# Graph network with sorted edges: digit counts before the first sort, pair counts behind it, a sixth of the records gathered later, and radial products over 128 rows

## The chip, the cores and the metric

One core of one Trainium2 chip. The time is that of one launch on the device in microseconds (us), the median of the runs shown. PE is TensorE, DVE VectorE, ACT ScalarE, POOL GpSimd, SP SyncE; SP issues most DMAs, POOL the indirect ones (gathers).

## What is computed

Four layers over a graph of 12,500 nodes with 32 features and 400,000 edges (src, dst). Each adds its result to x and normalizes the rows:

```python
edge_index = jnp.stack([src, dst])
x = _layernorm(x + gat(x, edge_index, w, fc_w, fc_b, bias))               # layer 0: attention, 4 heads
x = _layernorm(x + ratio(x, node_vec1, W, b, edge_index))                 # layer 1: weighted sums over edges
x = _layernorm(x + equivariant(x, edge_weight, edge_attr_3, edge_index))  # layer 2: radial weights per edge
x = _layernorm(x + gcn(x, edge_index, W1, b1, W2, b2))                    # layer 3: two convolutions
```

Layer 0 takes, for each edge, a logit from both ends, its maximum and sum over all edges of one src, and sums messages by src. Layer 2 computes for each edge a vector of 384 radial weights,

```python
R = jax.nn.relu(abs_distances[:, None] @ w1 + b1) @ w2 + b2   # 400,000 x 64 @ 64 x 384
```

multiplies it with spherical harmonics of the edge's vector and the features of its src, and sums by dst.

## The kernel before

Nodes are numbered in 98 windows (W) of 128 (the low 7 bits of a node number are its lane, the higher ones its window). Edges are brought into orders in which each tile of 128 edges has one window, so that sums over edges are matmuls with one-hot matrices. The kernel makes these orders itself, with six sorts of 128 x 4096 keys or of chunks, one before the gathers and five beside them:

1. `pair_counts` (DVE L1299 to L1329, PE L968 to L990): how many edges go from each window to each other. A step takes 16 columns of edges; DVE makes two one-hot tiles of 128 x 1568 for it (L1311), PE multiplies 16 pairs of 128 x 98 (L977) and adds one count to the semaphore `pairs_used`. Two buffers; DVE waits for `pairs_used` before it writes a buffer again. There are 196 steps. Then `window_tables` (PE L991) turns counts into the window of each group of edges: `win_src`, `win_nbr`, `win_dst` and `win_att`.
2. `source_list`: the first sort, by src. It inserts pads by `wpads` and needs the counts by source window alone.
3. Payloads of edges, weights, and the first node table `tab0` (37 columns), which SP sends to DRAM (`send_table(0)`, L491).
4. `id_list` (a sort), then `edge_list` 0 and 1, each one large sort and one of chunks. In a sort DVE compares and exchanges (L1449, L1450), and takes tiles that PE turned (L1016) out of the banks (L1492, L1514, L1517). PE adds one count to `turned_out` per 16 tiles.
5. Beside step 4: POOL gathers `tab0` rows of each edge's dst (L666, `gat<-tab,nbr`), 104 iterations of 4 slots of 8 gathers. ACT stores what came.
6. `segment_max` on DVE, with PE's turned tiles (L1056, L1714); then SP's wait for `seg_done` is over.
7. The attention pass, 416 steps (PE L1100, L1085, L1091; DVE L1843, L1817, L1862), and beside it POOL collects the records of edges in the order by dst (L645, `pay<-records`), 104 iterations of 4 x 8 gathers, where SP stores each slot to `by_dst` and loads the next numbers (L528, L530). Round 0 is issued ahead of `segment_max`, round 1 waits for `seg_done`.
8. Layer 1; then the radial pass, 416 steps: POOL gathers 8 tiles of features (L666, `gat<-tab,pay`) when SP has loaded the slot's `pay` from `by_dst` (the load waits for `step_done`), and computes geometry (L704 to L739); PE makes the hidden layer (L1195), ACT applies relu (L953) into `dsts`, PE multiplies by `w2p` (L1213), four times a pair of tiles in a step, DVE multiplies and reduces (L2086, L2091, L2097), PE sums (L1085).
9. Layer 3, with spreads and sums by edge lists.

Each engine runs its own program in the order in which it is written.

Of the kernel before, what the change touches and what calls it, by code (L numbers as in the profile page):

```python
# [14 lines left out]
P = 128  # L15
# [24 lines left out]
NT = NG * TILES_PER_GROUP  # L40
ROWS = P * NT

# [22 lines left out]
BLOCKS = M // GROUP  # L65
assert XROWS * M == CHUNKS * CHUNK_EDGES and QROWS * M == P * NT and XGPS * XTILES == TPS
# [9 lines left out]
HT = 16  # L76
BIG = float(2.0 ** 100)
# [62 lines left out]
def resnorm_gnn_kernel(nc, a, out):  # L140

    ctx = ExitStack()
    with ctx:
# [6 lines left out]
        def dram(name, shape):  # L150
# [34 lines left out]
                     for k in range(2)] for b in range(2)]  # L185
        pairs = [acc[0:W, k * W:(k + 1) * W] for k in range(2)]
# [21 lines left out]
        tmpi = sb("tmpi", [P, 1], I32)  # L208
        signs = sb("signs", [P, 7])
# [23 lines left out]
        pay = sb("pay", [P, SLOTS, TPS, 6])  # L233
        gat = sb("gat", [P, SLOTS, TPS, C0])
# [32 lines left out]
        hid = dsts[0:HID + 1, 0:2 * TPS * P].bitcast(F32).rearrange("p (b t n) -> p b t n", b=2, t=TPS)  # L267
# [16 lines left out]
        w2p = sb("w2p", [HID + 1, 384])  # L284
# [47 lines left out]
        consts = sem("consts")  # L332
        pairs_hot = sem("pairs_hot")
# [125 lines left out]
        def _(sp):  # L459
# [72 lines left out]
            def record_loads():  # L532
                with sp.Fori(1, ITERS) as i:
                    record_round(i, False, False)
                record_round(ITERS, False, True)

            def edge_loads(pas):
                with sp.Fori(0, ITERS) as i:
                    for s in range(SLOTS):
                        tiles = bass.ds(i * (SLOTS * TPS) + s * TPS, TPS)  # L540

                        sp.wait_ge(step_done, i * SLOTS + (BASE[pas] + s + 1))
                        sp.dma_start(payv(s, pas), by_dst_v[:, tiles, :]).then_inc(pay_in[s], 16)

            sp.wait_ge(listed, 1)
# [4 lines left out]
            send_table(0, tab0, C0)  # L550
            sp.wait_ge(listed, 2)
            sp.dma_start(ids_dst, sortA[:, 0:NT].bitcast(I32)).then_inc(ids_sent, 16)
            for k in range(2):
                sp.wait_ge(row_keys_made, k + 1)
                sp.dma_start(key_rows[k].rearrange("(p g) c -> p (g c)", p=P), row_keys).then_inc(row_keys_sent, 16)
            for s in range(SLOTS):
                sp.wait_ge(adst_out[s], 16 * ITERS)
            sp.wait_ge(row_keys_made, 3)
            sp.dma_start(arena[:, 0:NT * HEADS], adst_tiles).then_inc(seg_loaded, 16)
            sp.wait_ge(ids_sent, 16)  # L560
            record_round(0, True, False)
# [5 lines left out]
            for s in range(SLOTS):  # L567
                sp.wait_ge(rec_out[s], 16 * ITERS)
            edge_loads(PASS_L2)
# [19 lines left out]
        def _(pool):  # L589
# [44 lines left out]
            def collect():  # L634
# [16 lines left out]
                with pool.Fori(1, ITERS) as i:  # L651
                    step(i, False)

# [88 lines left out]
            def radial_gather():  # L742

                def step(i, s, gathers, geo):
# [16 lines left out]
                with pool.Fori(0, ITERS - 1) as i:  # L761
# [207 lines left out]
        def _(pe):  # L969
# [21 lines left out]
            def window_tables():  # L991
                pe.wait_ge(grouped, 1)
                t_.matmul(bank[2][0:W, 0:4], before[0:W, 0:W], wcount[0:W, :], start=True, stop=True).then_inc(ended, 1)
                for turn, lists in enumerate(((0, 1, 2), (3,))):
                    pe.wait_ge(compared, turn + 1)
                    b = 0
                    for k in lists:
                        parts = gge[k].shape[1] // (P * 3)
                        q = gge[k].shape[1] // parts
                        for part in range(parts):  # L1000
                            last = t_.matmul(bank[b][0:1, 0:q], ones[0:W, 0:1], gge[k][0:W, part * q:(part + 1) * q],
                                             start=True, stop=True)
                            b += 1
                    last.then_inc(tabled, 1)
# [33 lines left out]

            pair_counts()
            window_tables()  # L1040
            sort_turns(0, sortA, sortB, LOGM, QROWS, TILES_PER_GROUP)
# [163 lines left out]
            def radial_step(i, s, first, more):  # L1205
                n = i * SLOTS + s
                for p in range(TPS // 2):
# [4 lines left out]
                    for h in range(2):  # L1212
                        last = t_.matmul(bank[1 + 2 * (p % 2) + h][:, 0:384], hid[:, s % 2, 2 * p + h, :], w2p[:, :],  # L1213
# [29 lines left out]
        def _(dve):  # L1243
# [19 lines left out]
            dve.sem_inc(pairs_used, 2)  # L1263
            dve.sem_inc(spread_hot, SLOTS)
# [7 lines left out]
            v.memset(b1col[:, :], 1.0)  # L1272
            v.memset(prev_key[:, :], -1)
# [12 lines left out]
            v.tensor_copy(lanes[:, 0:1], lane[:, :])  # L1286
            v.tensor_scalar(wkey[:, 0:1], lane[:, :], 17, None, ALU.logical_shift_left)
# [9 lines left out]
            dve.drain()  # L1297

# [31 lines left out]

            def window_tables():
# [13 lines left out]
                v.tensor_reduce(wtotal[0:W, 3:4], pairs[0], AX.X, ALU.add)  # L1345
                dve.drain()
                for k, size in enumerate((P, P, GROUP, GROUP)):
                    v.tensor_scalar(wgroups[0:W, k:k + 1], wtotal[0:W, k:k + 1], float(size - 1), None, ALU.add)
# [844 lines left out]
```

## Time and profile before

| | |
|---|---|
| runs | 29,038.42, 29,043.08, 29,071.11 us (median 29,043.08) |
| profiled execution | 29,032.15 us, span 29,030.3 us |
| PE busy | 11,866.2 us (41%) |
| DVE busy | 17,276.3 us (60%) |
| POOL busy | 15,318.8 us (53%) |
| ACT busy | 4,732.5 us (16%) |
| mean granted clock of PE | 0.544 |

A row of a timeline gives start, duration, engine, line, operation, output and inputs with shapes, the count, and in brackets the idle time before it with what ended it. A row of stages gives its stretch, its length, busy time and number of instructions of each engine, the granted clock of PE (1.00 is 2.4 GHz, 0.50 is 1.2 GHz), the DMA share and GB/s. "remote" is a releaser outside the profile's engines and queues.

### The profile page before, as it was taken

Reading aid. Unit: us, or ns where it says so; the run is one execution under the profiler, and the core shown is the slowest. Engines: PE = TensorE matmul, PEld = TensorE weight load, DVE = VectorE, ACT = ScalarE, POOL = GpSimd, SP = SyncE. Lnnn points to the kernel's source line nnn. Section 1 sums busy time; section 2 is a strip of 40 time slices with the busy share of each in tenths; the row PEclk is TensorE's granted clock in tenths of the full one; section 3 lists DMA queues with packets and bytes.
Section 4 is the critical chain, followed back from the end, with each engine's and each line's share of the span. In section 5 each row is a group of like instructions: output and inputs, shape, how many; then the busy total and the mean of one; then the engine's idle time right before and its main releaser. Section 6 shows DMA issues by size and latency. Waiting matters only on the chain.

```text
span 29030.3 us, 271981 instructions
## 1 busy us (share of the span) xinstructions
PE 11866.2 (41%) x59822; PEld 8687.7 (30%) x59823; DVE 17276.3 (60%) x25029; ACT 4732.5 (16%) x11144; POOL 15318.8 (53%) x16979
## 2 busy tenths in 40 slices
PE   4000010000000000277743239999999996424422
PEld 3000010000000000266632125555555554313311
DVE  9986875774300000266634558888888886554555
ACT  0000000000000000022232004434434434201400
POOL 0028886876577777500002656666666662364166
PEclk9555555555555555577755555555555555555555
DMA  0011112112000000011155230000000004523623
GB/s 7 0 36 26 26 25 29 25 25 37 15 7 7 7 7 7 11 25 25 25 116 125 65 53 10 9 9 9 9 9 9 9 9 103 142 61 73 187 61 57
DMA packets 1778830, 1089.15 MB, mean 38 GB/s; under 512 B 930123, under 2 KB 1730348, under 8 KB 1777324
## 3 DMA queue, kind: packets, MB, share of 16 engines
q0 software_dynamic: 454272, 410.40, 9.6%
q1 hardware_dynamic: 827516, 358.86, 5.0%
q10 hardware_dynamic: 496944, 318.82, 4.7%
q8 instruction: 32, 0.52, 0.0%
q14 instruction: 66, 0.54, 0.0%
HBM read 697.54 MB, written 387.81 MB: 37 GB/s over the span
## 4 chain that ended last, share of the span: by engine, by line
PE 28%; another core or an unknown queue 15%; issue 13%; POOL 13%; DVE 13%; DMA 5%; DVEq 5%; ACT 3%; ACTq 3%; SPq 1%; POOLq 0%
PE banks L1213 16%; POOL gat L666 11%; PE banks L1085 9%; DMA dsts<-key_rows 3%; DVE hot L1806 3%; DVE arena L1817 2%; POOL srcs L686 2%; DVEq L450 2%; ACT dsts L953 2%; ACT srcs L883 1%; DVE arena L1449 1%; DVE arena L1311 1%; PE banks L1195 1%; DVE msg L1862 1%
## 5 line engine op out<-in xcount | busy, mean ns | idle before, releaser
L686 POOL DMA_INDIRECT srcs<-spread,nbx x2808 | 3086.2, 1099 | 6742.4 <-issue 4503.1
L666 POOL DMA_INDIRECT gat<-tab,nbr x3328 | 4074.2, 1224 | 3079.8 <-DMA tab<-arena 1926.8
L1213 PE MATMUL banks<-w2p,dsts 65*128 65x384 f32 x6656 | 4773.3, 879 | 597.7 <-ACT dsts L953 594.8
L666 POOL DMA_INDIRECT gat<-tab,pay x3328 | 3210.0, 965 | 2351.4 <-DMA pay<-by_dst 1410.1
L645 POOL DMA_INDIRECT pay<-records,nbr x3328 | 3530.7, 1061 | 1372.2 <-issue 1097.4
L1817 DVE TENSOR_TENSOR arena<-arena,banks 128x96 f32 (+3 forms) x6136 | 1539.5, 251 | 4376.3 <-remote 2516.0
L1016 PE MATMUL banks<-ident,arena 128*128 128x128 f32 x2240 | 425.9, 376 | 5679.4 <-DVE arena L1450 4555.1
L1213 PEld LDWEIGHTS banks<-w2p,dsts 65*128 65x128 f32 x6656 | 2013.1, 332 | 1895.1 <-issue 1201.6
L1085 PE MATMUL banks<-srcs,hot 128*128 128x96 bf16 (+1 forms) x11232 | 1165.2, 280 | 3425.5 <-DMA srcs<-spread,nbx 1746.8
L2097 DVE TENSOR_REDUCE red<-srcs 128x80 f32<-128x1280 f32 x1664 | 2474.5, 1487 | 151.8 <-issue 0.5
L1449 DVE TENSOR_TENSOR arena<-arena 128x1024 f32<-128x1024 f32 (+3 forms) x1548 | 2087.9, 1349 | 219.6 <-issue 149.0
L1016 PEld LDWEIGHTS banks<-ident,arena 128*128 128x128 f32 x2240 | 399.4, 202 | 5706.5 <-DVE arena L1450 4571.6
L1450 DVE TENSOR_TENSOR arena<-arena 128x1024 f32<-128x1024 f32 (+3 forms) x1548 | 2097.4, 1355 | 0.0
L1085 PEld LDWEIGHTS banks<-srcs,hot 128*128 128x128 bf16 x11232 | 872.1, 136 | 3718.7 <-DVE hot L1806 1614.9
L1898 DVE TENSOR_SCALAR hotT<-dsts,lanes 128x1024 bf16<-128x1024 uint8 x1404 | 1057.1, 753 | 1390.2 <-DMA dsts<-key_rows 1248.0
L1100 PE MATMUL banks<-nodesp,hotT 128*128 x3328 | 242.1, 174 | 3764.1 <-issue 2528.7
L1165 PE MATMUL banks<-arena,hotT 128*128 x11232 | 1179.9, 281 | 1374.7 <-DVE hotT L1898 1045.0
L2091 DVE TENSOR_TENSOR srcs<-banks,g_v 128x384 f32<-128x384 f32 x3328 | 1683.9, 548 | 0.0
L1085 PEld LDWEIGHTS banks<-red,hot 128*128 128x128 f32 x6656 | 1522.4, 333 | 257.4 <-issue 257.4
L1806 DVE TENSOR_TENSOR hot<-iota,key_dst 128x1024 bf16<-128x1024 f32 x936 | 1147.2, 1226 | 579.7 <-issue 579.6
L1085 PE MATMUL banks<-red,hot 128*128 128x41 f32 x6656 | 1445.7, 406 | 4.8 <-DVE red L2106 4.8
L1843 DVE TENSOR_REDUCE am<-banks 128x32 f32<-128x96 f32 x416 | 105.2, 253 | 2167.2 <-remote 1866.8
(343 smaller groups left out, 19406.0 us busy)
## 6 DMA issues: line engine op xcount, KB each, us to landing
spread<-srcs SPq DMA_DIRECT2D x936, 192.0 KB, 3.5
dsts<-key_rows SPq DMA_DIRECT2D x936, 128.0 KB, 3.6
spread<-srcs ACTq DMA_DIRECT2D x468, 204.0 KB, 4.1
staged<-gat ACTq DMA_DIRECT2D x416, 148.0 KB
gat<-staged ACTq DMA_DIRECT2D x416, 148.0 KB
dsts<-key_rows ACTq DMA_DIRECT2D x468, 128.0 KB, 4.6
gat<-tab,nbr POOLq DMA_INDIRECT x3328
pay<-records,nbr POOLq DMA_INDIRECT x3328
```

The lines of the kernel that those rows point to most:

```text
L645: pool.indirect_dma_start(out=pay[:, s, t, :], out_offset=None, in_=records, in_offset=bass.IndirectOffsetOnAxis(ap=nbr[:, s, t:t + 1], ax ...
L666: pool.indirect_dma_start(out=gatv(s, GC[pas])[:, t, :], out_offset=None, in_=TAB[pas], in_offset=bass.IndirectOffsetOnAxis(ap=row, axis=0 ...
L686: pool.indirect_dma_start(out=chunk_rows(s, c)[:, q, :], out_offset=None, in_=rows, in_offset=bass.IndirectOffsetOnAxis(ap=nbx[:, s, q:q + ...
L1085: last = t_.matmul(where(q), hots[:, t, :], rows(t), start=(h == 0), stop=(h == tiles - 1))
L1165: last = t_.matmul(bank[2 * (s % 2) + q][:, j * c3:(j + 1) * c3], hotT_row[s % 2][:, q * XGROUP + j:(q + 1) * XGROUP:CHUNK_EDGES], tabs[:, ...
L1213: last = t_.matmul(bank[1 + 2 * (p % 2) + h][:, 0:384], hid[:, s % 2, 2 * p + h, :], w2p[:, :], start=True, stop=True)
L1449: v.tensor_tensor(b[:, d, d, :, :, :], a[:, d, 0, :, :, :], a[:, d, 1, :, :, :], ALU.min)
L1450: last = v.tensor_tensor(b[:, d, 1 - d, :, :, :], a[:, d, 0, :, :, :], a[:, d, 1, :, :, :], ALU.max)
L1806: return v.tensor_tensor(dst, iota[:, :].rearrange("p (a n) -> p a n", a=1).to_broadcast([P, TPS, P]), key.rearrange("p (t a) -> p t a", a ...
L1817: last = v.tensor_tensor(dst, dst, where(q), ALU.add)
L2091: last = v.tensor_tensor(prod[:, pb, h, 16:40, :].rearrange("p (u o) k -> p u o k", o=3), bank[lo + h][:, 256:384].rearrange("p (u a k) -> ...
L2097: v.tensor_reduce(red[:, b, t0:t0 + 2, 0:40], prod[:, pb, :, :, :], AX.X, ALU.add)
```

## The change

Three parts.

- **Counts.** `source_counts` counts edges by source window alone, before the first sort. A window number is split into a high part (13 values) and a low digit (8). For 8 edges of a partition at a time a matmul of 104 x 64 counts all pairs, of which only those of the same edge are used (`digit_same`). 391 groups, in 23 steps of 17 matmuls: DVE writes 1,768 and 1,088 elements a step, with two buffers, and waits for `digits_used`. `source_windows` makes `win_att` from it. Then come the payloads, the weights and `tab0`, then `source_list`, then `pair_counts` (as before) and `window_tables` for the other three tables, then `id_list` and the rest. SP sends `tab0` before it waits for the first sort. SP issues round 0 of the collecting when the numbers are stored and the attention's inputs are out, ahead of its wait for the row keys.
- **Late records.** Collecting runs over 87 of the 104 iterations. The records of the other 17 (544 of 3,328 tiles) are gathered in the radial pass: in the first 68 iterations (272 of 416 steps) POOL issues two more gathers after the step's eight, into a tile `late`; SP stores them to `by_dst` and loads two columns of numbers per step.
- **128 rows.** The radial product takes `hid_rows` and `w2rows`, 128 rows, where it took 65. Rows 65 to 127 are zeros.

```diff
+LATE_ITERS = 17
+EARLY_ITERS = ITERS - LATE_ITERS
+LATE_TILES = 2
+LATE_ROUNDS = LATE_ITERS * TPS // LATE_TILES
...
+            def late_records(i, s, first):
+                pool.wait_ge(nbr_in[s], nbr_count(1, EARLY_ITERS + i))
+                if not first:
+                    pool.wait_ge(rec_out[s], i * 16 + 16 * EARLY_ITERS)
+                pool.nop(nofuse=True)
+                for t in range(LATE_TILES):
+                    pool.indirect_dma_start(
+                        out=late[:, s, t, :], out_offset=None, in_=records,
...
                         gather_step(PASS_L2, i + (s + 2) // SLOTS, s2, False)
+                    if with_late:
+                        late_records(i, s, first_late)
...
                     sp.wait_ge(step_done, i * SLOTS + (BASE[PASS_L2] + s + 1))
                     sp.dma_start(payv(s, PASS_L2), by_dst_v[:, tiles, :]).then_inc(pay_in[s], 16)
+                    if late_store:
+                        sp.wait_ge(rec_in[s], i * (16 * LATE_TILES) + 16 * TPS * EARLY_ITERS)
+                        sp.dma_start(by_dst_v[:, late_tiles(i - 1, s), :], late[:, s, :, :]).then_inc(rec_out[s], 16)
+                    if late_load:
+                        sp.dma_start(nbr[:, s, 0:LATE_TILES], ids_dst[:, late_tiles(i, s)]).then_inc(nbr_in[s], 16)
```

One step of DVE's `source_counts`:

```diff
+                def step(n, b):
+                    dve.wait_ge(digits_used, n + 1)
+                    at = bass.ds(n * (DSTEP * DIGITS), DSTEP * DIGITS)
+                    v.tensor_tensor(
+                        high_hot[b],
...
+                        ALU.is_equal)
+                    v.tensor_tensor(
+                        low_hot[b],
...
+                        ALU.is_equal).then_inc(digits_hot, 1)
```

PE's radial product:

```diff
-                        last = t_.matmul(bank[1 + 2 * (p % 2) + h][:, 0:384], hid[:, s % 2, 2 * p + h, :], w2p[:, :],
+                        last = t_.matmul(bank[1 + 2 * (p % 2) + h][:, 0:384], hid_rows[:, s % 2, 2 * p + h, :], w2rows[:, :],
```

The order on DVE (PE's calls are moved alike):

```diff
-            pair_counts()
-            window_tables()
-            source_list()
+            source_counts()
+            source_windows()
 
             dve.wait_ge(loaded, 16 * N_LOADS)
...
+            source_list()
+            pair_counts()
+            window_tables()
             id_list()
             edge_list(0, srcs, dsts, key_src, from_src)
             edge_list(1, dsts, srcs, key_dst, from_dst)
+            v.memset(hid_rows[HID:P, :, :, :], 0.0)
```

PE, from its start through the first sort, before, branches and register work left out (L977 is the pair counts, L1016 the tiles turned for a sort):

```order
L977 MATMUL banks<-arena 98x98 x16
L977 MATMUL banks<-arena 98x98 x5
L989 MATMUL banks<-ident,arena 98x98
L993 MATMUL banks<-wcount,before 98x4
L1001 MATMUL banks<-arena,ones 1x468 x4
L1001 MATMUL banks<-arena,ones 1x416 x8
L1016 MATMUL banks<-ident,arena 128x128 x448
L1035 MATMUL banks<-ident,arena 128x104 x32
```

Now, to the second sort (L1060 is the digit counts, L1042 the pair counts, L1100 and L1119 a sort; the loops of L1060 and L1042 have the same rows as one step):

```order
L1060 MATMUL banks<-arena 104x64 x34
L1073 MATMUL banks<-arena 104x8
L1078 MATMUL banks<-wcount,before 98x1
L1085 MATMUL banks<-arena,ones 1x416 x4
L1100 MATMUL banks<-ident,arena 128x128 x448
L1119 MATMUL banks<-ident,arena 128x104 x32
L1042 MATMUL banks<-arena 98x98 x16
L1042 MATMUL banks<-arena 98x98 x5
L1054 MATMUL banks<-ident,arena 98x98
L1078 MATMUL banks<-wcount,before 98x3
L1085 MATMUL banks<-arena,ones 1x468 x4
L1085 MATMUL banks<-arena,ones 1x416 x4
```

The pair counts stand between the first sort and the second, where POOL's gathers have begun.

POOL, a step in the loop of the radial pass before, branches and register work left out:

```order
L666 DMA gat<-tab,pay 128x32 x8
L704 TENSOR_TENSOR tmpA<-fT,rx 128x192
L705 TENSOR_TENSOR tmpB<-fT,rx 128x192
L706 TENSOR_TENSOR tmpC<-fT,rx 128x192
L730 CAST wparts<-pay 128x24
```

And now:

```order
L724 DMA gat<-tab,pay 128x32 x8
L707 DMA late<-records,nbr 128x6 x2
L762 TENSOR_TENSOR tmpA<-fT,rx 128x192
L763 TENSOR_TENSOR tmpB<-fT,rx 128x192
L764 TENSOR_TENSOR tmpC<-fT,rx 128x192
L788 CAST wparts<-pay 128x24
```

Two gathers of `late` follow the eight, ahead of the geometry of the same step.

## Rows read from the trace of the kernel before

**Rows 1.** The chain that ended last, shares of the span by engine.

```profile
PE 28%; another core or an unknown queue 15%; issue 13%; POOL 13%; DVE 13%; DMA 5%; DVEq 5%; ACT 3%; ACTq 3%; SPq 1%; POOLq 0%
```

**Rows 2.** Busy time by stage, all engines; clock, DMA share and GB/s last.

```profile
23.00:694.00 671.00, 306.38 (x3125) 274.94 (x3125) 670.02 (x393) 0.00 (x0) 24.19 (x13) 1.00 0.01 0
694.00:726.00 32.00, 15.18 (x27) 2.93 (x27) 15.72 (x46) 0.00 (x0) 0.00 (x0) 0.84 0.00 0
735.00:1709.00 974.00, 84.68 (x480) 80.82 (x480) 920.05 (x631) 0.00 (x0) 0.00 (x0) 0.54 0.00 0
1983.00:7211.00 5228.00, 367.44 (x1920) 343.78 (x1920) 3728.06 (x3086) 92.01 (x415) 4074.09 (x3328) 0.53 0.19 26
7525.00:12140.00 4615.00, 325.45 (x1665) 288.63 (x1666) 254.31 (x622) 86.44 (x172) 3500.49 (x3296) 0.51 0.08 7
12500.00:13500.00 1000.00, 754.63 (x4817) 696.77 (x4818) 691.67 (x1808) 244.47 (x489) 0.00 (x0) 0.77 0.10 25
17600.00:24400.00 6800.00, 6158.20 (x16827) 3911.41 (x16826) 5696.81 (x9340) 2708.28 (x7686) 4439.39 (x7233) 0.50 0.09 11
```

**Rows 3.** DVE alone, the five sorts beside the gathers: the first, and the sum.

```profile
1954.00:3139.00 1185.00, 921.00 (x627) 0.54 0.20 25
...
sum 5220.00, DVE 3756.37; mean DVE 751.27
```

**Rows 4.** DVE's waits: 735 to 1710 us, then 1950 to 7175 us (total, times, longest).

```profile
DVE arena L1492 <- PE banks L1016: 26.4, 7, 3.8
...
DVE arena L1517 <- remote: 528.1, 22, 43.1
```

**Rows 5.** Timelines of the maximum stage: PE, then DVE, then POOL's last gather.

```profile
7238.65 9.80 PE L1056 MATMUL banks<-ident,arena 128*104 128x128 f32 x72 [83.87 <-DMA arena<-adst_tiles]
...
7250.34 1.23 DVE L1714 COPY arena<-banks 104x1024 f32<-104x1024 f32 x1 [3.07 <-remote]
7257.39 1.23 DVE L1714 COPY arena<-banks 104x1024 f32<-104x1024 f32 x1 [5.82 <-remote]
7272.79 1.23 DVE L1714 COPY arena<-banks 104x1024 f32<-104x1024 f32 x1 [14.18 <-remote]
7284.70 9.14 DVE L1714 COPY arena<-banks 104x1024 f32<-104x1024 f32 x8 [10.69 <-remote]
...
7278.33 0.95 POOL L645 DMA_INDIRECT pay<-records,nbr  x1 [0.31 <-issue]
```

**Rows 6.** Timelines of one attention step beside the collecting: PE, then DVE.

```profile
8019.31 3.89 PE L1085 MATMUL banks<-msg,hot 128*128 128x133 f32 x16
...
8039.23 0.26 DVE L1843 TENSOR_REDUCE am<-banks 128x32 f32<-128x96 f32 x1 [41.85 <-remote]
...
8084.50 0.29 DVE L1817 TENSOR_TENSOR arena<-arena,banks 128x133 f32 x1 [42.64 <-remote]
```

**Rows 7.** L1862, one per attention step: 1,000 us beside the collecting, and after it.

```profile
8550.00:9550.00 1000.00, 13.82 (x11) 0.51 0.08 7
12500.00:13500.00 1000.00, 188.30 (x151) 0.77 0.10 25
```

**Rows 8.** POOL timeline: the first gather of the first table, and a late one.

```profile
1983.90 1.58 POOL L666 DMA_INDIRECT gat<-tab,nbr  x1 [1926.78 <-DMA tab<-arena]
...
7061.42 0.94 POOL L666 DMA_INDIRECT gat<-tab,nbr  x1 [0.30 <-issue]
```

**Rows 9.** Waits in the radial pass, 17600 to 24400 us (total, times, longest).

```profile
POOL gat L666 <- DMA pay<-by_dst: 1256.7, 401, 3.7
...
DVE srcs L2086 <- PE banks L1213: 355.4, 501, 0.9
```

**Rows 10.** PE timeline of a radial step: its first product, and the next step's.

```profile
20002.88 2.87 PE L1213 MATMUL banks<-w2p,dsts 65*128 65x384 f32 x4
...
20019.49 1.59 PE L1213 MATMUL banks<-w2p,dsts 65*128 65x384 f32 x2
```

More of the change, by code:

```diff
@@ L76 @@
 HT = 16
+DIGITS = 8
+HIGH = -(-W // DIGITS)
+DGROUPS = -(-TE // DIGITS)
+DSTEP = 17
+DSTEPS = DGROUPS // DSTEP
+assert DSTEP * DSTEPS == DGROUPS and DSTEPS % 2 == 1 and HIGH * DIGITS <= P
 BIG = float(2.0 ** 100)
@@ L233, in resnorm_gnn_kernel @@
         pay = sb("pay", [P, SLOTS, TPS, 6])
+        late = sb("late", [P, SLOTS, LATE_TILES, 6])
         gat = sb("gat", [P, SLOTS, TPS, C0])
@@ L742, in radial_gather, with step @@
             def radial_gather():
-                def step(i, s, gathers, geo):
+                def step(i, s, gathers, geo, with_late=False, first_late=False):
                     n = i * SLOTS + s
@@ L760, in radial_gather @@
                     geometry(0, 0, stage, first=True)
-                with pool.Fori(0, ITERS - 1) as i:
+                for s in range(SLOTS):
+                    step(0, s, True, True, True, True)
+                with pool.Fori(1, LATE_ROUNDS) as i:
+                    for s in range(SLOTS):
+                        step(i, s, True, True, True)
+                with pool.Fori(LATE_ROUNDS, ITERS - 1) as i:
                     for s in range(SLOTS):
@@ L989, in pair_counts, with source_counts, step @@
                 t_.transpose(bank[1][0:W, 0:W], pairs[0], ident[0:W, 0:W]).then_inc(pairs_turned, 1)
[L991 to L1004, printed above, removed]
+            def source_counts():
+                def step(n, b, first=False, last=False):
+                    pe.wait_ge(digits_hot, n + 1)
+                    for g_ in range(DSTEP):
+                        mm = t_.matmul(bank[0][0:HIGH * DIGITS, 0:DIGITS * DIGITS],
+                                       high_hot[b][:, g_, :, :].rearrange("p h t -> p (h t)"),
+                                       low_hot[b][:, g_, :, :].rearrange("p t l -> p (t l)"),
+                                       start=first and g_ == 0, stop=last and g_ == DSTEP - 1, skip_group_check=True)
+                    mm.then_inc(digits_used, 1)
+                step(0, 0, first=True)
+                with pe.Fori(0, (DSTEPS - 1) // 2 - 1) as i:
+                    step(i * 2 + 1, 1)
+                    step(i * 2 + 2, 0)
+                step(DSTEPS - 2, 1)
+                step(DSTEPS - 1, 0, last=True)
+                pe.wait_ge(digits_kept, 1)
+                t_.matmul(bank[1][0:HIGH * DIGITS, 0:DIGITS], high_same[0:HIGH * DIGITS, :], digit_sum[0:HIGH * DIGITS, :],
+                          start=True, stop=True).then_inc(digits_turned, 1)
@@ new lines, in window_tables @@
+            def window_tables(turn, lo, hi):
+                pe.wait_ge(grouped, turn)
+                t_.matmul(bank[2][0:W, 0:hi - lo], before[0:W, 0:W], wcount[0:W, lo:hi], start=True, stop=True).then_inc(ended, 1)
+                pe.wait_ge(compared, turn)
+                b = 0
+                for k in range(lo, hi):
+                    parts = gge[k].shape[1] // (P * 3)
+                    q = gge[k].shape[1] // parts
+                    for part in range(parts):
+                        last = t_.matmul(bank[b][0:1, 0:q], ones[0:W, 0:1], gge[k][0:W, part * q:(part + 1) * q],
+                                         start=True, stop=True)
+                        b += 1
+                last.then_inc(tabled, 1)
```

172 lines of the change are left out of this document (127 added, 45 removed).

## The prediction

> **What bounds the kernel now.** I read five views in this order: the chain that ended last, the busy time by stage, the timelines of three places, the waits, and the rows of single operations. A measurement of this kernel tells a change from none at about 0.2%, some 60 us.
>
> The chain [rows 1] names no engine that holds the end: PE has 28%, DVE and POOL 13% each, and 15% stand under "another core or an unknown queue". This program has one core, so that entry is a gap of explanation, and it matters below. The stages [rows 2] say what each stretch is made of: 671 us of pair counts with DVE busy throughout; 974 us of the first sort with DVE busy 920; then 5,228 us in which POOL issues the 3,328 gathers of the first table while DVE does five more sorts; 4,615 us in which POOL collects the records, DVE busy only 254; the attention at its own speed; and the radial pass, with PE busy 6,158 of 6,800 us at clock 0.50.
>
> The reader is to see one thing in the second and third of these. DVE's five sorts beside the gathers have 3,756 us of work and take 5,220; the sort alone has 920 and takes 974 [rows 2, 3]. DVE isn't slower at work (921 against 920), it waits: L1517 waits 528 us in 22 waits for a "remote" releaser, the longest 43 us, where alone such a wait is for PE and under 4 us [rows 4]. What remote is, the next two places show. In the maximum stage PE turns tiles while POOL issues 32 gathers: PE has done 72 of its 128 matmuls by 7248.45, enough for nine of DVE's sixteen copies, but DVE makes its sixth at 7250.34, the seventh at 7257.39, the eighth at 7272.79, and all that is left from 7284.70 on, just after POOL's last gather [rows 5]. So the counts that PE sends arrive late and one by one while POOL issues gathers without a pause, and freely once it stops. In the attention PE finishes L1085 at 8023.20, and DVE takes its sums at 8084.50, released "remote" [rows 6]. Each attention step has four such counts and takes 1000/11 = 90 us beside the collecting, and 1000/151 = 6.6 us without it [rows 7]; 90/4 = 22.5 us for each count, and at 44.8 us per 32 gathers (4,615 us for 103 iterations) that is a count every 16 gathers. DVE's own counts to PE, and DMA's, show no such delay.
>
> **The change part by part.**
>
> *Digit counts in place of pair counts before the first sort.* 23 steps of 1,768 + 1,088 elements. L1311 takes 670.02/393 = 1.70 us for 1,568 [rows 2], 1.09 ns an element, so 3.1 us a step, 72 us, and with four passes over 3,125 columns and small work some 100. Gone from ahead of the sort are 671 + 32 us [rows 2]. The table's transfer now leaves before the sort instead of after it, which hides 39 us. POOL's first gather comes at 1983.9 [rows 8]; now at 1984 - 703 - 39 + 100 + 15 (numbers stored and loaded) = 1,357.
>
> *The pair counts beside the gathers.* This is the term that decides. Their 196 steps each need one count from PE before the buffer is free. Alone a step takes 3.4 us. Beside gathers I price a count at 16 gathers. With DVE mostly idle a gather takes 0.94 + 0.30 = 1.25 us [rows 8]; with some disturbance I take 1.30, so 20.8 us, times 196 = 4,077, and the pair counts end at 5,434. The gathers end at 1,357 + 3,328 x 1.30 = 5,683. The tables take 28 us, and then come the five sorts, nearly all of them without gathers: 3,756 us of work and some 55 us of waits each as in the sort alone (974 - 920) = 4,030, plus 50 for the first 220 us. They end at 5,434 + 28 + 4,080 = 9,542, where they ended at 7,174 before: **+2,370 us**. Bounds: if counts cost 15 us, 2,940 for the pair counts, and the sorts are mixed, about +1,500; if gathers are slow at 1.40 and the pair counts hold to their end (6,017), +2,850. I take the 16 gathers since the attention held this pace for 4,600 us. POOL's first round of collecting now runs ahead of the maximum stage instead of beside it: the copies of [rows 5] take no 45 us, -30 us.
>
> A rule of the Trainium skill speaks here. "SBUF — State Buffer", section "SBUF: two separate sides", says that the vector engine and GpSimd share a port pair under an exclusive lock, each blocking the other for whole instructions. The trace agrees in part: a gather takes 5,228/3,328 = 1.57 us beside the sorts and 1.25 alone, but the waits of [rows 5] have no vector work beside them. By that rule alone the pair counts would cost about their 671 us, which is the second case below.
>
> *A sixth of the records late.* 17 of 104 iterations leave the collecting: 17 x 44.8 = -762. The attention does one step per 90 us there, so 8.5 steps come later at 6.6 us: +56. **-705 us**. In the radial pass POOL issues two more gathers in 272 of 416 steps, 2 x 1.26 = 2.5 us each; POOL waits 1256.7/401 = 3.1 us a step for the pay load [rows 9], which hides them with 0.6 us to spare. SP's additional store and load lie in its waits. If that cover were gone it would cost up to 2.5 us x 272 = 680.
>
> *The radial products over 128 rows.* A step takes 16.61 us (20002.88 to 20019.49 [rows 10]) and PE is its bound, at clock 0.50. Clock 1.00 was granted to the pair counts, 128 rows, though PE was busy 306 of 671 us, and 0.77 to the attention, also mostly 128 rows; the radial pass, busier than both, has 65 rows and 0.50 [rows 2]. So the rows used seem to count, and I expect the clock to rise for much of the pass. What it gives is small: DVE waits for PE only 355.4 us in the pass [rows 9], 0.87 us of each of 409 steps; then DVE is the bound. 0.87 x 144 plus, where POOL is now at 16.61 - 3.13 + 2.5 = 16.0 and some tenths, 0.4 x 272: 125 + 109, rounded down to **-200 us**. Bounds: nothing if the clock stays, -360 if all 416 steps gain 0.87.
> The Trainium skill ("TensorE: Matmul & The Clock Gate", Part 1) has the clock follow how busy PE has been lately. By that rule alone the pass, 91% busy, would be at the full clock already, which [rows 2] contradict; padding would then give 0 in place of -200.
>
> *Small edits* (memsets, masks, the order of SP's waits) come to a few us, beside other work.
>
> Sum against the profiled execution, 29,032 us (11 below the median of the runs): 29,032 + 2,370 - 30 - 705 - 200 = **30,467, say 30,470**.
>
> **The rivals.**
>
> 1. *The counts come promptly, faster.* The late counts may need what sorts and attention have and the pair counts have not. Then the pair counts take 671 us beside the gathers and DVE reaches the sorts at 2,056. The gathers end at 1,357 + 5,228 = 6,585; until then the sorts go at 5,220/4,030 = 1.295 of their quiet time, 3,497 of 4,030 done, and end at 7,118. That is only 56 us earlier than now, since the gathers move earlier and DVE becomes the bound. 29,032 - 56 - 30 - 705 - 200 = 28,041; 28,240 without the clock. For it: at the start of the sorts some counts pass at once, and in the radial pass, with 8 gathers and then a pause, all of them. Against it: three kinds of PE work wait alike [rows 4 to 6]. The point from which it decides: the first part pays for the rest as long as it costs under 905 us, which in the same working is about 10 us a count.
> 2. *Two steps per release, no change.* The pair counts are double-buffered. If a release passes both, they take 98 x 20.8 = 2,038 us and end at 3,395; with gathers to about 6,180 the sorts have done 2,130 of 4,030 by then and end at 8,081, +907. 29,032 + 907 - 30 - 905 = 29,004. Against it: in [rows 5] four counts were due at 7250 and passed singly.
> 3. *The late gathers disturb the radial pass.* Ten gathers in a row instead of eight, and hardly a pause: if one count of PE in a step comes 2 us late, 272 x 2 = +544, and the forecast becomes 31,014. The pause shrinks from 6.6 to 4 us, so it isn't excluded.
> 4. *The clock stays at 0.50.* +200 in every case: 30,670 with the forecast.
>
> **How the numbers follow.** Throttled pair counts: 0.60 (case 3 takes 0.05 of it, case 4 a third); prompt: 0.30; in between: 0.10, of which 0.04 end below by over 0.2%, 0.04 within it and 0.02 above. The likeliest time is 30,470, and its own range 29,800 to 31,000: +1,500 or +2,850 in the first part, and 0 to -360 in the last. Since the prompt case holds three in ten, the range has to reach it: 27,950 to 31,000. Faster 0.30 + 0.04 = 0.34; same 0.04; slower 0.60 + 0.02 = 0.62.
>
> **What the profile after would show.** First gather near 1,357. L1311's successor beside the gathers, in pairs with waits near 20 us and "remote" as releaser, PE hardly busy: right; back to back at 3.4 us a step: case 1. Five sorts with waits under 4 us and ending near 9,540. Collecting over 87 iterations, some 3,900 us. In the radial pass clock above 0.50, the wait of PE for ACT gone, POOL's wait for the pay load near 0.5 us, a step near 16.0. The prediction is wrong if the pair counts end long before the gathers do.

## The result, and the profile after

The changed kernel takes 28,533.56 us (median of 4 runs, 28,496 to 28,577), the kernel before 29,044.83 on the same chip: ratio 0.9823, interval 0.9806 to 0.984. That is 511 us faster, where 1,430 us slower was forecast; the time lies inside the wide range and far outside the likeliest case's own.

The first view is the chain of waits of the changed kernel; [rows 1] answer to it.

```profile
DVE 33%; DVEq 16%; issue 16%; another core or an unknown queue 15%; PE 8%; DMA 5%; POOL 3%; ACT 3%; ACTq 1%; SPq 1%; POOLq 0%
```

PE has left the chain (28% before, 8% now), DVE has taken its place. The 15% of an unknown queue have stayed.

The busy time by stage, columns as in [rows 2]: the digit counts, the pair counts, the five sorts, the attention beside the collecting and after it, and the radial pass with late gathers and without.

```profile
23.00:110.00 87.00, 39.17 (x393) 36.03 (x393) 84.71 (x56) 0.00 (x0) 21.11 (x13) 1.00 0.08 1
1348.00:2012.00 664.00, 304.66 (x3106) 273.35 (x3107) 664.00 (x391) 10.64 (x48) 545.24 (x390) 0.50 0.16 24
2040.00:7020.00 4980.00, 366.66 (x1916) 342.78 (x1916) 3759.13 (x3111) 80.94 (x365) 3713.41 (x2947) 0.53 0.17 24
7313.00:11122.00 3809.00, 270.85 (x1384) 240.79 (x1384) 202.01 (x515) 69.09 (x140) 2953.10 (x2737) 0.51 0.08 7
11200.00:13600.00 2400.00, 1815.77 (x11525) 1677.08 (x11525) 1657.05 (x4321) 584.61 (x1170) 0.00 (x0) 0.77 0.10 25
16600.00:21400.00 4800.00, 2621.39 (x10665) 1667.93 (x10663) 3597.27 (x5980) 1702.20 (x4940) 3360.71 (x5205) 0.76 0.08 9
21700.00:23700.00 2000.00, 1251.89 (x5089) 796.12 (x5087) 1721.88 (x2863) 815.47 (x2367) 1368.62 (x2239) 0.80 0.10 10
```

The second row decides: the pair counts took 664 us beside the gathers, with DVE busy in all 664, and not the 4,077 forecast. Their clock is 0.50 here, where [rows 2] had 1.00, and that costs nothing, because PE needs 305 of 664 us. The timelines inside it, DVE, then PE, then POOL:

```profile
1599.77 13.70 DVE L1457 TENSOR_TENSOR arena<-iota,arena 128x1568 bf16<-128x1568 f32 x8
...
1599.91 1.57 PE L1042 MATMUL banks<-arena 128*98 128x98 bf16 x16 [1.84 <-DVE arena L1457]
...
1606.09 1.39 POOL L724 DMA_INDIRECT gat<-tab,nbr  x1 [0.30 <-issue]
1607.78 1.40 POOL L724 DMA_INDIRECT gat<-tab,nbr  x1 [0.31 <-issue]
1609.49 1.40 POOL L724 DMA_INDIRECT gat<-tab,nbr  x1 [0.30 <-issue]
```

DVE makes its tiles back to back, 1.71 us each, and POOL's gathers start every 1.70 us, where the late gather of [rows 8] takes 0.94 + 0.30 = 1.25: one gather for one operation of DVE. PE's counts come in time for every step, since DVE has no gap.

Where the 519 us between the two profiled executions went, by first and last instructions of the stages:

| stage | before | after | difference |
|---|---|---|---|
| start to `seg_done` | 7,507 | 7,276 | -231 |
| first attention step | 7,550 | 7,313 | -6 more |
| attention pass | 7,004 | 6,311 | -693 |
| layer 1 to the radial pass | 2,845 | 2,864 | +19 |
| radial pass | 6,905 | 7,329 | +424 |
| the rest | 4,726 | 4,694 | -32 |

The first gather starts at 1,335 (1,984 before), the last ends at 6,702 (7,211), and the sorts end at 7,022 (7,174). The radial pass got longer though its clock rose from 0.50 to 0.76. DVE's L2254, four in a step, as columns of one line (DVE's busy time, clock, DMA share, GB/s):

```profile
16600.00:21400.00 4800.00, 1546.66 (x1040) 0.76 0.08 9
21700.00:23700.00 2000.00, 739.31 (x498) 0.80 0.10 10
```

4,800/260 = 18.5 us a step with late gathers, 2,000/124.5 = 16.1 without; 16.61 before [rows 10]. DVE's longest waits in the first stretch (total, times, longest), and one step's timelines of PE, POOL and DVE:

```profile
DVE arena L1974 <- remote: 703.4, 260, 3.1
```

```profile
18994.91 1.87 PE L1171 MATMUL banks<-red,hot 128*128 128x41 f32 x16
...
18998.63 0.95 POOL L707 DMA_INDIRECT late<-records,nbr  x1 [0.30 <-issue]
...
19001.71 0.20 DVE L1974 TENSOR_TENSOR arena<-arena,banks 128x41 f32 x1 [2.71 <-remote]
```

PE's sums are done at 18,996.78, POOL's tenth gather in a row at 18,999.58, and DVE takes the sums at 19,001.71. Each step waits 703.4/260 = 2.7 us there. In the steps without late gathers (21,700 to 23,700 us) that wait is all but gone:

```profile
DVE arena L1974 <- remote: 12.7, 13, 1.7
```

### The profile page after: what moved, and what is told of

Same layout as the page of the kernel before. It is cut to its first block, busy times and chain, and to the rows that moved or that the text cites. A ratio compares the mean times of both kernels' runs of the same rounds, so it can differ in the third digit from the quotient of the medians.

```text
span 28510.6 us, 274421 instructions
## 1 busy us (share of the span) xinstructions
PE 9785.8 (34%) x60217; PEld 7387.7 (26%) x60218; DVE 17317.6 (61%) x25094; ACT 4687.8 (16%) x11144; POOL 15512.2 (54%) x16979
## 4 chain that ended last, share of the span: by engine, by line
DVE 33%; DVEq 16%; issue 16%; another core or an unknown queue 15%; PE 8%; DMA 5%; POOL 3%; ACT 3%; ACTq 1%; SPq 1%; POOLq 0%
DVE arena L1603 7%; DVEq L2253 6%; PE banks L1171 5%; DVE red L2254 4%; DVE srcs L2248 4%; DVE arena L1974 3%; DMA dsts<-key_rows 3%; DVE hot L1963 3%; DVEq L1678 3%; POOL srcs L744 3%; DVEq L480 2%; DVE srcs L2243 2%; DVE arena L1604 2%; ACT srcs L948 1%
## 5 line engine op out<-in xcount | busy, mean ns | idle before, releaser
L724 POOL DMA_INDIRECT gat<-tab,nbr x3328 | 4262.3, 1281 | 2385.2 <-DMA nbr<-nbr_src 1280.6
L1299 PE MATMUL banks<-w2rows,dsts 128*128 128x384 f32 x6656 | 3417.6, 655 | 3132.7 <-ACT dsts L1018 2934.3
L692 POOL DMA_INDIRECT pay<-records,nbr x2784 | 2998.1, 1077 | 1422.6 <-issue 881.5
L1299 PEld LDWEIGHTS banks<-w2rows,dsts 128*128 128x128 f32 x6656 | 1517.9, 253 | 4085.0 <-DVE srcs L2248 3146.7
L2254 DVE TENSOR_REDUCE red<-srcs 128x80 f32<-128x1280 f32 x1664 | 2474.6, 1487 | 151.5
L1100 PE MATMUL banks<-ident,arena 128*128 128x128 f32 x2240 | 426.3, 376 | 5435.9 <-DVE arena L1604 4934.2
L1100 PEld LDWEIGHTS banks<-ident,arena 128*128 128x128 f32 x2240 | 399.6, 202 | 5464.1 <-DVE arena L1604 4952.9
L948 ACT CAST srcs<-banks 128x768 bf16<-128x768 f32 (+1 forms) x1404 | 1139.4, 812 | 1380.5 <-PE banks L1251 1114.0
L1251 PEld LDWEIGHTS banks<-arena,hotT 128*128 128x128 bf16 x11232 | 882.4, 139 | 1681.2 <-issue 1681.2
L2243 DVE TENSOR_TENSOR srcs<-banks,g_s 128x512 f32<-128x512 f32 x1664 | 1139.7, 685 | 210.7 <-issue 137.1
```

The source lines that it names most:

```text
L692: pool.indirect_dma_start(out=pay[:, s, t, :], out_offset=None, in_=records, in_offset=bass.IndirectOffsetOnAxis(ap=nbr[:, s, t:t + 1], ax ...
L724: pool.indirect_dma_start(out=gatv(s, GC[pas])[:, t, :], out_offset=None, in_=TAB[pas], in_offset=bass.IndirectOffsetOnAxis(ap=row, axis=0 ...
L1251: last = t_.matmul(bank[2 * (s % 2) + q][:, j * c3:(j + 1) * c3], hotT_row[s % 2][:, q * XGROUP + j:(q + 1) * XGROUP:CHUNK_EDGES], tabs[:, ...
L1299: last = t_.matmul(bank[1 + 2 * (p % 2) + h][:, 0:384], hid_rows[:, s % 2, 2 * p + h, :], w2rows[:, :], start=True, stop=True)
L2254: v.tensor_reduce(red[:, b, t0:t0 + 2, 0:40], prod[:, pb, :, :, :], AX.X, ALU.add)
```

## The experiments

All of them are the changed kernel with one edit, but the first, which is the kernel before with one.

**Two conditions.** One fact has to be told first, since the numbers can't be read without it. The runs were measured in six groups (e1 to e4; e5 to e8; e9 to e11; e12 to e14; e15 and e16; e17 and e18), and the groups fell into two kinds, the same for all kernels of a group: in the first, as in the result above, the kernel before took 28,987 us; in the five later ones it took 24,522 to 24,568. The attention shows the difference. The changed kernel's L2019, one per step, beside the collecting, in the result's trace and in one of the other kind (e9):

```profile
8550.00:9550.00 1000.00, 15.22 (x12) 0.51 0.08 7
```

```profile
7900.00:8900.00 1000.00, 189.09 (x151) 0.78 0.17 30
```

12 steps in 1,000 us against 151. In every trace of the first kind these steps lie some 90 us apart in the median, in every one of the second 6.7 to 6.8. The chain of e9 also has no entry for an unknown queue, which had 15% above:

```profile
POOL 35%; issue 20%; DVE 16%; PE 10%; DVEq 6%; DMA 5%; ACT 5%; ACTq 1%; POOLq 1%; SPq 1%
```

I call the kinds "late counts" and "prompt counts". Kernels of different groups are compared only within a kind, and by their ratios to the kernel before, which was measured anew in each group.

| run | edit | before | this | ratio (interval) |
|---|---|---|---|---|
| first group, late counts | | 28,987 | | |
| e1 | kernel before, 128 rows alone | | 28,741 | 0.9911 (0.9894 to 0.9927) |
| e2 | no late gathers | | 28,512 | 0.9835 (0.9818 to 0.9851) |
| e3 | window numbers in PSUM | | 31,552 | one run |
| e4 | pair counts first, no digit counts | | 28,610 | 0.9869 (0.9853 to 0.9886) |
| the other groups, prompt counts | | | | |
| e9 | the changed kernel | 24,558 | 23,546 | 0.959 (0.9574 to 0.9606) |
| e5, e10, e12, e15 | late gathers behind the geometry | 24,522 to 24,568 | 23,516 to 23,560 | 0.959, 0.959, 0.9583, 0.9593 |
| e6, e13, e16 | pause after 8 gathers | the same | 24,127 to 24,186 | 0.9837, 0.9845, 0.9848 |
| e8, e11, e14 | pause after 16 gathers | the same | 23,809 to 23,856 | 0.9706, 0.9717, 0.9709 |
| e7 | pause after 8, no late gathers | 24,522 | 24,775 | 1.01 (1.0083 to 1.0117) |
| e17 | window numbers in PSUM | 24,561 | 23,372 | 0.9517 (0.9498 to 0.9536) |
| e18 | pair counts first, no digit counts | 24,561 | 23,918 | 0.974 (0.9724 to 0.9756) |

### Why the pair counts weren't late: e3

```diff
-                            iotaw.rearrange("p (a w) -> p a w", a=1).to_broadcast([P, tiles, W]),
+                            bank[3][:, 0:W].rearrange("p (a w) -> p a w", a=1).to_broadcast([P, tiles, W]),
...
+                v.tensor_copy(bank[3][:, 0:W], iotaw)
+                dve.drain()
                 step(0, 0, HT)
```

> The changed kernel, but the pair counts' one-hot operations on DVE read the window numbers from a PSUM bank instead of SBUF, so they have one SBUF input in place of two. Same work on PE, same counts. Theory A: PE's counts come late only while POOL issues gathers unhindered, and it was DVE's operations with two SBUF inputs that held POOL to one gather per operation (1.70 us each) and let the counts pass. Then gathers here go at 1.25 to 1.4 us, DVE waits 10 to 20 us for counts, and the pair counts take 1,500 to 4,000 us. Theory B: the counts of this loop are prompt by their kind (bf16 products, a busy PE), whatever DVE reads. Then the loop stays at 660 to 750 us, whatever the pace of the gathers.

The busy time of the loop (all engines, as above), DVE's L1457 alone until the last gather and after it, DVE's waits, and three timelines: DVE (its last row stands behind the last gather), PE, POOL.

```profile
1348.00:6128.00 4780.00, 305.52 (x3117) 274.20 (x3118) 676.08 (x392) 92.13 (x416) 3143.58 (x3324) 0.50 0.18 28
...
1348.00:6042.00 4694.00, 600.17 (x346) 0.50 0.18 29
6042.00:6128.00 86.00, 75.91 (x46) 0.50 0.05 3
```

```profile
DVE arena L1457 <- remote: 3006.2, 111, 42.1
DVE arena L1457 <- issue: 1081.0, 30, 42.1
DVE arena L1457 <- PE banks L1042: 16.7, 7, 3.0
```

```profile
3012.63 3.49 DVE L1457 TENSOR_TENSOR arena<-banks,arena 128x1568 bf16<-128x1568 f32 x2 [41.29 <-issue]
3057.44 3.49 DVE L1457 TENSOR_TENSOR arena<-banks,arena 128x1568 bf16<-128x1568 f32 x2 [41.33 <-issue]
...
6052.09 75.95 DVE L1457 TENSOR_TENSOR arena<-banks,arena 128x1568 bf16<-128x1568 f32 x46 [13.40 <-remote]
...
3016.17 1.57 PE L1042 MATMUL banks<-arena 128*98 128x98 bf16 x16 [43.21 <-DVE arena L1457]
...
3000.89 0.94 POOL L724 DMA_INDIRECT gat<-tab,nbr  x1 [0.30 <-issue]
3002.14 0.94 POOL L724 DMA_INDIRECT gat<-tab,nbr  x1 [0.30 <-issue]
```

The same products on PE, the same 392 operations of DVE and the same work in them (676 us against 664), and the loop takes 4,780 us: 24.4 us a step. POOL's gathers start every 1.25 us in a row (every 1.41 with the pauses, 1,333 to 6,042 us for all 3,328), and PE waits 43 us for DVE, which waits for a count of PE. While gathers go, 173 steps (346 operations) take 27 us each; the last 23 follow each other without a gap once POOL has stopped, with the same operand in PSUM, so it isn't the read from PSUM that makes counts late. Theory A holds, though the loop takes longer than the 1,500 to 4,000 us it gave; B is out. It is one execution, but it lies 3,000 us from the changed kernel, whose four runs spread over 81 us. This is the forecast's own picture (4,077 us); it needed one operand moved out of SBUF to come true.

### Is it the kernel or the condition: e17

The same kernel as e3.

> The changed kernel with the window numbers of the pair counts in PSUM, again. If late counts belong to the chip and not to the kernel, then on a chip that runs the kernel before in 24,560 us the loop takes 665 to 700 us (4,780 on the first chip) with DVE never waiting 10 us, POOL's gathers beside it go at 1.25 us in place of 1.70, some 140 more of them get done in the loop, and the time is within 150 us of the changed kernel's 23,546. If the loop by itself makes the counts late, it takes 4,000 us and more here too, and the time is above 26,000.

DVE's longest wait in the loop, and timelines of DVE and POOL:

```profile
DVE arena L1474 <- PE banks L1042: 1.0, 1, 1.0
```

```profile
1599.80 13.66 DVE L1457 TENSOR_TENSOR arena<-banks,arena 128x1568 bf16<-128x1568 f32 x8
...
1600.69 0.94 POOL L724 DMA_INDIRECT gat<-tab,nbr  x1 [0.30 <-issue]
1601.94 0.94 POOL L724 DMA_INDIRECT gat<-tab,nbr  x1 [0.30 <-issue]
```

With prompt counts the loop takes 663 us, gathers go at 1.25 us beside DVE's unbroken work, the last gather ends at 6,436 in place of 6,616 (e9), and this version is the fastest of all: 0.9517 against 0.959, some 180 us (within 150 was expected). The same file is 3,000 us slower than the changed kernel where counts are late. So for counts to be late two things are needed: the condition of the group, and POOL issuing unhindered. How a POOL that is held lets counts pass isn't shown.

### What the first part is worth: e4 and e18

DVE, and PE alike (SP sends the table after the sort again):

```diff
-            source_counts()
+            pair_counts()
+            v.tensor_reduce(wtotal[0:W, 3:4], pairs[0], AX.X, ALU.add)
+            dve.drain()
             source_windows()
+            window_tables()
+            source_list()
...
-            source_list()
-            pair_counts()
-            window_tables()
             id_list()
```

> The changed kernel with the pair counts ahead of the first sort as before, no digit counts, and the table sent after the sort: the late records and the 128 rows alone. By the stages of the two traces the first part brought 231 to 237 us (end of the maximum stage 7,507 to 7,276). So the time should be 28,533 + 237 = 28,770 us, between 28,720 and 28,830. Rival: the first part brought only what the earlier start of round 0 of the collecting did (SP's order, some 30 us); then the time is 28,560 to 28,620.

> The late records and the 128 rows without the first part, again. On the first chip the first part was worth 0.46% (133 us), since the gathers and DVE's five sorts are nearly coupled. On a chip without late counts the sorts wait for nothing but work, so DVE's end bounds less: if the earlier gathers then bring what they are earlier by, 0.959 becomes 0.98 (400 to 600 us); if DVE's work bounds the stage, the first part brings 50 to 150 us here too and the ratio is 0.961 to 0.966.

Late counts: 0.9869 - 0.9823 = 0.0046, 133 us. The expected 28,770 was missed by 160 us, and 28,610 lies in its rival's range (28,560 to 28,620). The trace decides against the rival: the maximum stage ends at 7,502, 226 us later than in the changed kernel, as expected. Its attention pass and radial pass are 47 and 34 us shorter, which I can't explain; the kernel before, too, was 58 us faster in this group (28,987) than beside the changed kernel (29,045). Prompt counts: 0.974 - 0.959 = 0.015, 370 us; the maximum stage ends at 7,335 against 6,879 (e9). Between the two cases that were expected for e18 (50 to 150, and 400 to 600), and nearer the second; it seems that where the sorts have no late counts, more of the 650 us by which the gathers start earlier is kept. DVE's longest kinds of wait for the same line beside the gathers point to it, the changed kernel with late counts, then with prompt ones:

```profile
DVE arena L1671 <- remote: 408.0, 18, 42.4
```

```profile
DVE arena L1671 <- PE banks L1100: 8.6, 20, 0.7
```

### What the late records are worth: e2

```diff
-LATE_ITERS = 17
+LATE_ITERS = 0
...
-                for s in range(SLOTS):
-                    step(0, s, True, True, True, True)
-                with pool.Fori(1, LATE_ROUNDS) as i:
...
+                with pool.Fori(0, ITERS - 1) as i:
```

(SP's loops are changed alike.)

> The changed kernel with all 104 iterations of the collecting in the attention pass and no late gathers. Theory: ten gathers in a row hold back PE's sums by 2.7 us in each of 272 radial steps. Without them the radial pass takes 6,650 us in place of 7,356 (-700) and the attention pass 7,010 in place of 6,316 (+694): the time is within 60 us of the changed kernel's 28,533. Rival: the late gathers cost nothing and the digit counts or the 128 rows slow the radial pass; then it stays near 7,350 and the time is near 29,200.

0.9835 against 0.9823: no difference that the intervals allow to be told. The attention pass takes 6,993 us (6,311 with late gathers, so they bring 682), the radial pass 6,684.2 (7,328.5, so they cost 644). DVE's L2243, four in a step, in that trace, and POOL's wait for the pay load, in the changed kernel (16,600 to 21,400 us) and in e2 (17,400 to 23,600):

```profile
17400.00:23600.00 6200.00, 2292.99 (x1542) 0.80 0.06 10
...
POOL gat L724 <- DMA pay<-by_dst: 684.1, 260, 2.9
POOL gat L718 <- DMA pay<-by_dst: 994.0, 385, 2.9
```

6,200/385.5 = 16.1 us a step. Late gathers cost 2.4 us in each of 272 steps, as much as two gathers of 1.25 take. POOL waits 2.6 us a step for the load in both. With prompt counts they cost less. L2254 in e9, with late gathers and without, and DVE's wait for PE's sums there (12,500 to 16,700 us):

```profile
12500.00:16700.00 4200.00, 1501.95 (x1010) 0.77 0.09 10
17100.00:19000.00 1900.00, 706.32 (x475) 0.81 0.08 10
...
DVE arena L1974 <- PE banks L1171: 15.8, 61, 0.3
```

16.6 against 16.0 us: 0.6 a step, or 170 us in all. POOL has the same work in both conditions, so its work alone accounts for 0.6 of the 2.4 us at most, and the other 1.8 go with late counts. The semaphore events in the traces, which no view above shows, say where: with late counts PE's sums are counted 1.9 to 2.1 us behind the last of the ten gathers (nine in ten of 260 steps), some 1.6 behind the last of eight in e2, and never amid a row; in e9 they are counted amid the row, as soon as PE is done.

### What the 128 rows are worth: e1

```diff
-                        last = t_.matmul(bank[1 + 2 * (p % 2) + h][:, 0:384], hid[:, s % 2, 2 * p + h, :], w2p[:, :],
+                        last = t_.matmul(bank[1 + 2 * (p % 2) + h][:, 0:384], hid_rows[:, s % 2, 2 * p + h, :], w2rows[:, :],
```

(The tiles of 128 rows and their zeros come with it, as in the changed kernel.)

> The kernel before with the radial product over 128 rows alone. In the changed kernel the last 144 radial steps, which have no late gathers, took about 16.0 us against 16.6. If the rows do that and nothing else, all 416 steps take 16.0 us, the granted clock of the radial pass is 0.75 to 0.8, the pass takes 6,650 us in place of 6,933, and the time is 28,750 to 28,800 us. Rival: the faster clock is what slowed the 272 steps with late gathers to 18.4 us (PE finishes in other places of POOL's stream); then steps of 17 us or more show up here too and the time is 29,100 or above.

DVE's reduction (L2101 there), four in a step:

```profile
17600.00:23600.00 6000.00, 2220.18 (x1493) 0.80 0.06 10
```

16.1 us a step at clock 0.80, the radial pass 6,683 us (6,905 before): -222; by the ratio the kernel gains 0.9%, 258 us. The rival, a faster clock that disturbs the steps, is out.

### Where the late gathers stand: e5, and again e10, e12, e15

```diff
-                    if with_late:
-                        late_records(i, s, first_late)
                     for stage in range(4):
...
+                    if with_late:
+                        late_records(i, s, first_late)
```

> The changed kernel with the two late gathers of a radial step behind POOL's geometry instead of right behind the eight. Theory A: POOL's unbroken row of gathers holds PE's sums, so its length sets when DVE gets them; with eight in a row the 272 steps go back from 18.4 to 16.1 us, the late gathers fill POOL's wait for the pay load, the radial pass takes about 6,700 us in place of 7,330, and the time is about 600 us under the changed kernel's. Theory B: it is POOL's total work per step (16.0 us and the landing of pay) that bounds the steps; then the place doesn't matter and the time stays within 100 us of the changed kernel's.

> The changed kernel once more, beside the next two. The chip of the last four runs ran the kernel before in 24,522 us, and PE's counts reached DVE at once all through the collecting (attention steps of 6.6 us); the chip of the four runs ahead took 28,987. On a chip with late counts: 0.982 of the kernel before, about 28,480 to 28,550 us. On a chip without: the late gathers cannot hold PE's counts back and the first part brings its 600 us of earlier gathers, so between 23,500 and 23,900 us, 0.96 to 0.975.

> The late gathers behind POOL's geometry, again, now beside the changed kernel itself. On a chip with late counts, theory A (length of POOL's row): radial steps with late gathers of 16.1 us in place of 18.4, 600 us under the changed kernel. Theory B (POOL's total work): within 100 us of it. On a chip without late counts: within 100 us of it by both.

All four fell on groups with prompt counts. There the place makes no difference: 23,551 against 23,546 us side by side (e10, e9), and the radial pass takes 6,825 us against 6,827. For that condition theory A and B both say so. With late counts the place stays untried. That the length of POOL's row, and not its total work, holds most of the 2.4 us is read from the traces (under e2), not shown by an edit.

### A pause in POOL's row: e6, e7, e8, and again e11, e13, e14, e16

```diff
                             ).then_inc(rec_in[s], 16)
+                        pool.wait_ge(rec_in[s], i * (16 * TPS) + 16 * TPS)
```

(e8: only where `s % 2`.)

> The changed kernel; in the collecting POOL waits for each slot's eight records to land before it issues the next eight. Theory A (PE's counts pass when POOL's row is broken): attention steps beside the collecting fall from 90 us to 30 us or less, so about 130 to 300 of them are done beside it in place of 43; the collecting itself gets longer, from 44.8 us a round to 50 to 56; the attention pass gets shorter by 300 to 1,500 us, and so does the kernel. Theory B (counts are paced by the number of gathers, one every 16, wherever POOL pauses): steps take 100 us or more, the collecting takes 500 to 900 us longer, and the kernel is slower by about as much.

> As the paced collecting, with all 104 rounds beside the attention and no late gathers. Theory A: if the paced collecting hides most of the attention, 17 more rounds of about 52 us cost 880 us, less 17 rounds' attention steps, and the radial pass gets 640 us back: within 200 us of the paced kernel with late gathers. Theory B: slower than the changed kernel by 600 us or more.

> As the paced collecting, but POOL waits for a landing after every second slot only (16 gathers in a row, then a pause). Theory A with a count let through in each pause: between the changed kernel and the paced one, attention steps beside the collecting of 45 to 90 us. If every pause lets all counts that are due through, and the first microseconds of a row too, steps of 25 to 45 us. Theory B: steps of 90 us or more and a slower kernel.

Prompt counts again, so these show only the price: the collecting takes 4,853 us (e13) in place of 4,076 (e9), and nothing is gained, since the attention is hidden beside it at 6.6 us a step already. e6 and e8 ended 2.6% and 1.2% behind the changed kernel, e7 behind the kernel before. I had expected a gain, or a loss with attention steps of 90 us and more (theory B). The loss came (580 us for e6 against e9), but with steps under 7 us, so it decides nothing between the two. What a pause brings where counts are late is open.

## Why the prediction was wrong

**The first gather**: 1,357 forecast, 1,335 measured. Right; the digit counts' whole stretch took 87 us (23 to 110) where 100 were taken.

**The pair counts: the step that failed.** It was "Beside gathers I price a count at 16 gathers." All three places from which that price came have DVE waiting or reading banks of PSUM, while POOL takes 1.25 to 1.4 us a gather. The pair counts have DVE at work without a break on two SBUF operands, and that holds POOL to one gather per operation. e3 takes the second SBUF operand away and leaves the rest of the loop as it is: then the price is about right, 27 us a step beside gathers (24.4 over the whole loop) against 20.8 forecast, 19 gathers of 1.41 us in place of 16 of 1.30. So the mechanism was there, and the condition under which it acts was wrong. The trace of before had the sign of it: DVE's sort operations beside the gathers stretched these from 1.25 to 1.57 us on average. I read that as a cost to POOL alone. That counts come one by one is what e3 shows in the main: DVE waits 111 + 30 + 7 = 148 times in the 173 steps beside gathers. Case 2 (two steps per release, 10.4 us a step) is out. The time of case 1, in which counts are prompt, is what the forecast's range was stretched for; the measured time lies in the range for that reason, and not for its likeliest case. One bound was added up wrong, without effect: pair counts that hold to 6,017 give +2,900, not +2,850.

Of the Trainium skill, "SBUF — State Buffer", section "SBUF: two separate sides", says that an operation of DVE with two SBUF inputs and one of GpSimd that reads SBUF exclude each other for whole instructions. The gathers at 1.70 us beside operations of 1.71, and at 1.25 once an operand is in PSUM (e17), agree with it. The prediction weighed it as a rival to late counts. It was the thing that switches them off here.

**The sorts**: case 1 had them end at 7,118 and the maximum stage 86 us earlier. They ended at 7,022, and the stage at -231. The case was right that DVE becomes the bound and much of the gathers' 509 us earlier end is lost (231 are kept); it overrated DVE's waits (1,464 us of 5,220 before, 1,221 of 4,980 now).

**The late records beside the attention**: -705 forecast, -693 in the traces, -682 by e2. Right.

**The late records in the radial pass: the second step that failed.** It was that POOL's wait for the pay load "hides them with 0.6 us to spare". The wait did not shrink: it is 684.1/260 = 2.6 us a step, as in e2 without late gathers. It is no slack of POOL. The load is asked for when DVE's step is done, and that step became longer: DVE waits 2.7 us for PE's sums. Case 3, "if one count of PE in a step comes 2 us late, 272 x 2 = +544", names the place and nearly the size (2.4 us by e2, +644), but had a chance of 0.05. With this the second part brings 682 - 644 = 38 us where 705 was forecast.

**The 128 rows**: the clock rose to 0.76 to 0.80, and the pass gains 222 us by e1, 200 forecast. Right. The Trainium skill ("TensorE: Matmul & The Clock Gate", Part 1) has the clock follow how busy PE has been; e1 changes only the rows used and lifts it to 0.80 for the pass that stood at 0.50 before with PE busy 91% of it. The measurement decides.

The sum with the measured terms: 29,030 - 237 - 693 + 644 - 222 - 11 for the rest = 28,511, the changed kernel's span. The forecast had +2,370 - 30 where -237 was measured, and nothing where +644 was. The two errors work against each other, so the total is nearer than its first part.

## What to carry to other kernels

Before pricing a wait from another place of the trace, look at what the other engines do there that could switch the mechanism off; here it was whether DVE's operation reads SBUF twice. A wait for a load isn't slack if the load is asked for by the engine that the added work delays. And a measured ratio can belong to a condition of the machine: this change is worth 1.8% in one and 4.1% in the other, and its fastest variant in one (e17) is the slowest in the other (e3), so of the two the kernel whose DVE work holds POOL is the safe one.

## What the runs showed of the hardware that was not expected

- The same kernel before took 28,987 us in the first group and 24,568 us in the fourth, on the same chip (number 10). The changed kernel's traces show what differs: whether PE's counts to DVE pass while POOL issues gathers, with attention steps of 90 us or 6.8 us. What sets the condition is open; it isn't the kernel, as all kernels of a group share it, and not the chip alone. The result and the first group, with late counts, came first in time.
- With late counts, a count passes at once while DVE's operations on two SBUF operands hold POOL (664 us for the loop of 196 counts), and comes late when POOL runs free: DVE waits 148 times, 28 us on average and 42 at most (4,780 us for the same loop).
- Moving one of two operands of a DVE operation from SBUF to PSUM costs DVE nothing (13.66 against 13.70 us for eight) and takes POOL from 1.70 to 1.25 us a gather.
- 63 rows of zeros raise the clock: 0.50 to 0.80 for the radial pass, 6,905 to 6,683 us.
